# A routed MoE and attention kernel: dense batches get a place of their own, GpSimd makes the expert stages' rows, and all orders are planned anew

## The reference

```python
x = x + 0.5 * ffn(layernorm(x))      # stage A
x = x + attn(layernorm(x))           # stage B
x = x + 0.5 * ffn(layernorm(x))      # stage C, with the weights of stage A
```

## Time and profile before

| | |
|---|---|
| median of 3 runs | 1219.44 us (1216.77 to 1219.6) |
| profiled execution, its own time | 1225.29 us |
| its span, first to last instruction | 1223.5 us |
| PE, ACT, DVE, POOL busy | 94%, 78%, 59%, 55% |
| mean granted clock of PE | 0.946 of 2.4 GHz |
| DMA | 202 MB, mean 165 GB/s |

### The profile page before, as it was taken

How to read it: one execution, slowest core, us unless ns; L and a number is a source line. 1 busy time by engine, 2 the same in 40 slices (tenths; PEclk the granted TensorE clock), 3 DMA queues, 4 the chain that set the end, 5 groups by cost and what they waited for, 6 DMA issues and landing times.

```text
span 1223.5 us, 25810 instructions
## 1 busy us (share of the span) xinstructions
PE 1150.6 (94%) x8142; PEld 762.4 (62%) x8142; DVE 724.7 (59%) x2254; ACT 958.0 (78%) x2383; POOL 678.9 (55%) x768
## 2 busy tenths in 40 slices
PE   7989898999989989999999999999999999999896
PEld 3666576666666545676666665665766446667575
DVE  4775438666496745665555867555756636647245
ACT  4457748789898898997888888898989888888532
POOL 2035548537370887803876777881820884257646
PEclk8977888799999979999999998999999989999988
DMA  8056546456574115655677645567652144676872
GB/s 279 10 206 192 162 144 193 126 156 202 158 214 147 55 39 177 208 172 157 200 215 228 194 139 164 186 201 206 183 157 60 41 151 125 182 214 176 250 253 80
DMA packets 159882, 202.05 MB, mean 165 GB/s; under 512 B 16938, under 2 KB 103426, under 8 KB 159747
## 3 DMA queue, kind: packets, MB, share of 16 engines
q1 hardware_dynamic: 144196, 168.90, 44.8%
q0 software_dynamic: 15360, 31.49, 8.9%
q10 hardware_dynamic: 192, 0.02, 0.0%
HBM read 152.50 MB, written 47.84 MB: 164 GB/s over the span
## 4 chain that ended last, share of the span: by engine, by line
PE 68%; ACT 20%; DVE 4%; issue 3%; POOL 3%; DMA 2%; SPq 0%; POOLq 0%; ACTq 0%; DVEq 0%
PE psum L1568 63%; ACT probs L1173 7%; ACT psum L1182 6%; PE psum L1686 2%; DVE neg_m L1522 2%; POOL Y L1100 2%; ACT xnC L1138 1%; DMA wt<-packed 1%; ACT xnA L1138 1%; PE psum L1653 1%; ACT hg L1219 1%; POOL pause L1064 1%; ACT xnB L1138 1%; PE psum L1751 1%; ACT xg_T L1247 1%
## 5 line engine op out<-in xcount | busy, mean ns | idle before, releaser
L1522 DVE TENSOR_REDUCE neg_m<-psum 128x1 f32<-128x512 f32 x512 | 317.5, 685 | 189.4 <-PE psum L1568 188.9
L1568 PE MATMUL psum<-nat 32*128 32x512 f32 x2048 | 372.7, 667 | 2.8 <-ACT nat L1251 1.5
L1182 ACT ACTIVATE psum<-psum,neg_m 128x512 f32<-128x512 f32 x512 | 340.9, 681 | 34.5 <-DVE neg_m L1522 33.7
L1173 ACT ACTIVATE probs<-psum 128x512 f32<-128x512 f32 x512 | 266.0, 627 | 37.7 <-PE psum L1568 36.4
L1080 POOL DMA_INDIRECT slots_A<-xnA,posA x120 | 117.1, 976 | 197.9 <-DMA xs<-slots_A 64.3
L1100 POOL DMA_INDIRECT Y<-results_C,posC x120 | 115.4, 962 | 170.8 <-DMA results_C<-ys 130.9
L1064 POOL MEMSET pause<- 128x900 f32 x240 | 207.6, 865 | 0.1
L1568 PEld LDWEIGHTS psum<-xg_T,wt 128*128 128x128 f32 x1296 | 163.6, 200 | 49.7 <-ACT psum L1182 14.7
L1568 PEld LDWEIGHTS psum<-nat 32*128 32x128 f32 x2048 | 135.7, 191 | 91.7 <-issue 22.1
L1568 PE MATMUL psum<-xg_T,wt 128*128 128x128 f32 x1296 | 180.2, 290 | 7.4 <-DMA wt<-packed 3.3
L1568 PEld LDWEIGHTS psum<-wt,hg 128*128 128x128 f32 x1296 | 153.0, 193 | 27.6 <-ACT hg L1219 9.6
(11 more groups left out here) (190 smaller groups left out, 1374.9 us busy)
## 6 DMA issues: line engine op xcount, KB each, us to landing
wt<-packed SPq DMA_DIRECT2D x324, 320.0 KB, 4.0
xs<-slots_A SPq DMA_DIRECT2D x36, 256.0 KB, 4.3
results_A<-ys SPq DMA_DIRECT2D x36, 256.0 KB
xs<-slots_C SPq DMA_DIRECT2D x36, 256.0 KB, 4.4
results_C<-ys SPq DMA_DIRECT2D x36, 256.0 KB
X<-in_L_attn_x_dram SPq DMA_DIRECT2D x16, 256.0 KB, 8.0
out_dram<-X SPq DMA_DIRECT2D x16, 256.0 KB, 3.9
packed<-probs SPq DMA_DIRECT2D x1, 2560.0 KB, 9.0
```

What stands on the lines that cost most here:

```text
L1173: act.activation(probs[:, kt, j, :], at.banks()[j][:], ACT.Exp).then_inc(a_done, 1)
L1182: act.activation(at.banks()[j][:], at.banks()[j][:], ACT.Exp, bias=neg_m[:, g, n, j:j + 1], accum_out=sums[:, g, n, j:j + 1]).then_inc(S[" ...
L1522: V_.tensor_reduce(neg_m[:, g, n, j:j + 1], at.banks()[j][:], AX.X, ALU.max, negate=True).then_inc(S["r_done"], 1)
L1568: return nc.tensor.matmul(dst, w, m, start=start, stop=stop)
```

## The change

1. A dense batch's turned rows get a place of their own: `xT_F` has XF_RING + 1 places, the last for dense batches. A routed batch no longer waits for the dense one, and in the planner the dense batch takes `xTf_dense` instead of `xTf`.
2. In stages A and C the four tiles of rows are made by POOL, with `tensor_scalar` (times `rstd`, plus `shift`), and counted on a new semaphore `rows_done`. ACT keeps `scaled` for stage B alone. Who waited for `xn_done` of A or C now waits for `rows_done`: PE's `xTf`, ACT's next `norm`, DVE's next `scaled`.
3. The fill stands only between two `scat` or `gat` steps that follow each other on POOL. Where a row step stands between them, there is none: 212 fills in place of 240.
4. The planner's costs for `scat` and `gat` on POOL go from 3.4 to 2.4, the gap from 3.6 to 3.4, and the whole table of wanted times is new. So all lists are new.

```diff
-PERIOD, FIRST_B = 55.8, 402.13
+PERIOD, FIRST_B = 54.81, 448.4
...
-GAP = 3.6
+GAP = 3.4
...
+    "rows": ((("DVE", 1.0), ("POOL", 1.9)), 0.0),
...
-    "rank2": ((("PE", 1.0), ("DVE", 4.6)), 0.0), "scat": ((("POOL", 3.4),), 3.0),
+    "rank2": ((("PE", 1.0), ("DVE", 4.6)), 0.0), "scat": ((("POOL", 2.4),), 3.0),
...
-            steps[s, b, "xTf", 0].takes.append("xTf")
+            steps[s, b, "xTf", 0].takes.append("xTf_dense" if c == DENSE[s] else "xTf")
...
-                steps[s, c, "dh", EXPERTS * UNITS - 1].gives.append((0, "xTf"))
+                steps[s, c, "dh", EXPERTS * UNITS - 1].gives.append((0, "xTf_dense"))
...
-        xT_F = sb("xT_F", [P, XF_RING, TOKENS])
+        xT_F = sb("xT_F", [P, XF_RING + 1, TOKENS])
...
+        def xTf_place(s, b):
+            return XF_RING if CHUNK_OF[s][b] == DENSE[s] else xTf_turn[s, b] % XF_RING
...
-            def apart():
-
-                linked(pool.memset(pause[:], 0.0))
+            after_pair = {step for old, step in zip(order["POOL"], order["POOL"][1:]) if old[2] in ("scat", "gat")}
+
+            def apart(at):
+
+                if at.step in after_pair:
+                    linked(pool.memset(pause[:], 0.0))
...
+            def scaled(at):
+
+                s, b = at.stage, at.index
+                pool.wait_ge(S["shift_done"], at.count("shift_done"))
+                if b >= XN_RING:
+                    old = b - XN_RING
+                    if CHUNK_OF[s][old] == DENSE[s]:
+                        pool.wait_ge(a_full, at.count("a_full", "xTf", index=old))
+                    else:
+                        pool.wait_ge(scat_in[s][old % XN_RING], scattered(s, old))
+                for n in range(TILES):
+                    last = pool.tensor_scalar(xn[s][:, xn_place(s, b) + n, :], X[:, b % X_RING, n, :], rstd[s][:, n:n + 1],
+                                              shift[s][:, n:n + 1], ALU.mult, ALU.add)
+                last.then_inc(S["rows_done"], 1)
...
                 act.wait_ge(S["mv_done"], at.count("mv_done"))
-                wait(act, S["xn_done"], at.count("xn_done", "scaled", index=at.index - 1))
+                made = "xn_done" if at.stage == "B" else "rows_done"
+                wait(act, S[made], at.count(made, "scaled", index=at.index - 1))
...
-                pe.wait_ge(S["xn_done"], at.count("xn_done", "scaled", 0))
+                pe.wait_ge(S["rows_done"], at.count("rows_done", "scaled", 0))
```

More of the change, by code:

```diff
@@ L191 @@
     "y": ((("PE", 1.75), ("DVE", 0.65)), 0.0), "ystore": ((("SP", 0.48),), 4.2),
-    "gat": ((("POOL", 3.4),), 3.0), "comb": ((("DVE", 2.6),), 0.0), "store": ((("SP", 0.48),), 2.5),
+    "gat": ((("POOL", 2.4),), 3.0), "comb": ((("DVE", 2.6),), 0.0), "store": ((("SP", 0.48),), 2.5),
     "weights": ((("SP", 6.5),), 3.0), "b2": ((("PE", 1.9), ("ACT", 0.48)), 0.0), "cen": ((("PE", 2.0), ("DVE", 0.75)), 0.0),
@@ L213, in __init__ @@
         self.key, self.wanted, self.name = key, wanted, name
-        self.parts, self.lag = PARTS[name]
+        self.parts, self.lag = PARTS["rows" if name == "scaled" and key[0] != "B" else name]
         self.banks = GROUP if name in ("max", "rmax", "s") else 1
@@ L439, in plan @@
 def plan(steps):
-    free = {"xnA": XN_RING, "xnC": XN_RING, "xTf": XF_RING, "Y": Y_RING, "route": 1, "xs": XS_RING, "xg": XG_RING,
+    free = {"xnA": XN_RING, "xnC": XN_RING, "xTf": XF_RING, "xTf_dense": 1, "Y": Y_RING, "route": 1, "xs": XS_RING, "xg": XG_RING,
             "w": W_QUADS, "hg": HG_RING, "dhg": DHG_RING, "ys": YS_RING, "d": D_MOST, "a": A_MOST, "r": M_MOST}
@@ L677 @@
     "xn_done": {"scaled": 1},
+    "rows_done": {"scaled": 1},
     "lg_done": {"top1": 1},
@@ L733, in macaron_kernel @@
     comb_turn = {batch: i for i, batch in enumerate(combs)}
-    xTf_turn = {st[:2]: i for i, st in enumerate(st for st in order["PE"] if st[2] == "xTf")}
+    xTf_turn = {st[:2]: i for i, st in enumerate(st for st in order["PE"] if st[2] == "xTf" and CHUNK_OF[st[0]][st[1]] != DENSE[st[0]])}
     xTf_order = list(xTf_turn)
@@ L1125, in scaled @@
             def scaled(at):
-                s, b = at.stage, at.index
+                b = at.index
                 act.wait_ge(S["shift_done"], at.count("shift_done"))
-                if s != "B" and b >= XN_RING:
-                    old = b - XN_RING
-                    if CHUNK_OF[s][old] == DENSE[s]:
-                        act.wait_ge(a_full, at.count("a_full", "xTf", index=old))
-                    else:
-                        act.wait_ge(scat_in[s][old % XN_RING], scattered(s, old))
-                if s == "B":
-                    wait(act, d_full, at.count("d_full", "xT", index=b - 1))
+                wait(act, d_full, at.count("d_full", "xT", index=b - 1))
                 for n in range(TILES):
-                    last = act.activation(xn[s][:, xn_place(s, b) + n, :], X[:, b % X_RING, n, :], ACT.Identity,
-                                          bias=shift[s][:, n:n + 1], scale=rstd[s][:, n:n + 1])
+                    last = act.activation(xn["B"][:, n, :], X[:, b % X_RING, n, :], ACT.Identity,
+                                          bias=shift["B"][:, n:n + 1], scale=rstd["B"][:, n:n + 1])
                 last.then_inc(S["xn_done"], 1)
@@ L1230, in xTf @@
             def xTf(at):
-                i = xTf_turn[at.stage, at.index]
-                if i >= XF_RING:
-                    s0, b0 = xTf_order[i - XF_RING]
+                s, b = at.stage, at.index
+                if CHUNK_OF[s][b] != DENSE[s] and xTf_turn[s, b] >= XF_RING:
+                    s0, b0 = xTf_order[xTf_turn[s, b] - XF_RING]
                     act.wait_ge(d_full, counts["d_full", (s0, b0, "logits", 0)])
-                    if CHUNK_OF[s0][b0] == DENSE[s0]:
-                        act.wait_ge(a_full, counts["a_full", (s0, CHUNK_OF[s0][b0], "dh", EXPERTS * UNITS - 1)])
-                act.activation(xT_F[:, i % XF_RING, :], a_bank(at)[:], ACT.Copy).then_inc(a_done, 1)
+                act.activation(xT_F[:, xTf_place(s, b), :], a_bank(at)[:], ACT.Copy).then_inc(a_done, 1)
             def xg(at):
@@ L1351, in scaled @@
                 plus = shift[at.stage]
-                wait(dve, S["xn_done"], at.count("xn_done", index=at.index - 1))
+                made = "xn_done" if at.stage == "B" else "rows_done"
+                wait(dve, S[made], at.count(made, index=at.index - 1))
                 chain(V_.tensor_tensor(plus[:], mv[at.stage][:, :, 0], r[:], ALU.mult))
```

30 lines of the change are left out of this document (15 added, 15 removed).

## The result

| | before | after |
|---|---|---|
| median of the runs | 1219.52 us (4 runs) | 1189.89 us (4 runs, 1187.95 to 1193.21) |
| ratio | 1 | 0.9761, 95% interval 0.9729 to 0.9792 |
| the profiled execution, its own time | 1225.29 us | 1187.95 us |
| its span | 1223.5 us | 1186.2 us |
| mean granted clock in it | 0.946 | 0.978 |

The change makes the kernel faster by 29.6 us. The forecast was 1205 us, a gain of 14.5. The sign held, and the range (from 1188) just so; the gain is twice the forecast's.

The account below looks back on a forecast made before the run. PE was taken as the bound, with its 72.9 us of idle time and its time below full clock to be had. Terms +2.5 - 6 - 9 - 2 = -14.5 us gave 1205 us, range 1188 to 1225.

Parts of the forecast that it names:

- What bounds the kernel: Whole kernel: PE busy 94% of the span; to be had are its 72.9 us idle and its time below full clock.
- Part 1, price on POOL: Rows on POOL: 0.28 us per row tile, four 1.1 us (0.5 to 2.1); POOL stays near 690 us, free as load.
- Part 2, first batch: First rows wait behind POOL's setup, PE begins at 10.9 instead of 8.3 us, delay passed on: +2.5 us (1.9 to 3.5).
- Part 3, the start: Dense place, 60 to 110 us: two PE idles covered, first scatter and expert quads earlier: -6 us (0 to -19).
- Part 4, the middle: Behind 110 us: a third of the 26 us that ACT's rows hold in the chain, -9 us (0 to -26).
- Part 5, the tail: Before the tail's gathers: fewer xloads ahead of the store of chunk 11's last results, -2 us (0 to -4).
- The port: SBUF port shared by POOL and DVE: rows could hold up weighted sums, at most 2 us worse; counted as nothing.
- ACT was the bound in full: Rival, middle: all 26 us of ACT's rows in the chain come back, 1188 us; chance 0.14.
- Hidden anyway: Rival: ACT's work was already hidden, middle 0, start -4, tail 0, first batch +2.5: 1218 us, no change; chance 0.15.
- Rows stuck in POOL's line: Rival, behind the start: row steps wait behind POOL's gathers and scatters and stop PE, +23 us to 1228; chance 0.16.

Follow-up runs that it names:

- s_first_again: The changed kernel with batch 0's rows made inside POOL's setup, ahead of its affine_selects, run beside the change: 0.9726 of before, the change 0.9727.
- o_old_lists: The kernel before with its own lists, only the expert stages' rows moved from ACT to POOL, no fill where a row step stands between pairs: 0.9966 of before.
- l_act_load: The changed kernel, lists kept, with four unread 128x128 passes added on ACT behind each norm of A and C: 0.9838 of before.

## Why the prediction was right in sign and too small

**What bounds the kernel.** I named two things to be had, PE's idle time and the time below full clock, and then priced every part but one by idle time and chain. Idle time fell by 2.7 us of 72.9; the gain stands in the 80 us less at 1.2 GHz.

**Part 1, price on POOL.** 0.45 us where I took 0.28; inside the bounds, and nearest to the row I had called the upper one. It cost nothing: POOL is at 60%, and its rows wait for DVE's shift far more than anyone waits for them.

**Part 2, first batch.** +3.2 us at PE's first transposes, at 11.50 instead of 8.34 us, where I had +2.5 within 1.9 to 3.5. But I said that it is passed on to the end. In `s_first_again`, which takes it back, the product of span and clock falls by 3 us and the clock gives most of it away, so that no gain is seen at the end.

**Part 3, the start.** The mechanism was right in each step: rank1 and rank2 between the dense matmuls, both waits gone, scatter at 62.97 (forecast near 65), quads at 86.48. The size was 6, less 2.5 for the first batch, and some 13 came. The clock was in my bounds, up to 13.5 us "if all the clock loss goes too", and not in the sum. Time at 1.2 GHz up to 260 us fell from 71.6 to 34.1 us, worth 18.8, and its idle time there rose by 4.3. The idle time of 60 to 110 us stayed at 5.7 of 50 (5.9 before), because the wait for xnB came: what I had counted as won there was lost again, and the gain came by the clock.

**Part 4, the middle: the step that failed.** The step is the term for the clock, which I put at nothing. I took a third of the 26 us of ACT's rows in the chain, -9, from PE's idle time, and wrote that the trace can't say whether one order drifts less than another. The idle part was about right: PE's idle time from 260 to 1110 us fell from 28.2 to 21.3, 7 us, and `o_old_lists` gets 5.5 of them with no new order at all. But the middle gave some 24. The missing term is the clock: 44.4 us at 1.2 GHz became 3.4, worth 20.5. It was in the earlier trace rows, a clock of 0.98 over 900 us, which is 18 us to be had, beside 30.7 of idle time, and I gave it no term. `o_old_lists` shows that the lighter ACT alone does not bring it, and `l_act_load` that the new lists keep only part of it once ACT has half of its load again, 30.7 us at 1.2 GHz. It takes both. The new order I called a part of this term and gave no price. The planner's own lengths, 1196.8 and 1175.5 us, could have given one: 21 us, though for costs that differ a little.

**Part 5, the tail.** Nothing came, where I had -2 within 0 to -4: 66.5 us from the last `wo` add in both, and the first gather equally far from the end.

**The port.** The weighted sums of A take 349 ns, 346 before, beside 56 us of rows on POOL. The rule of the Trainium skill, "SBUF — State Buffer", section "SBUF: two separate sides", would let the new rows hold them up, or be held up by them. The trace agrees where the two meet, which is at five row passes and ten sums. There it is mostly the rows that wait: 0.47 to 0.83 us instead of 0.44, 0.8 us in all.

```profile
L1123 POOL TENSOR_SCALAR xnC<-X,rstdC,shiftC x64: 437/442/833, 160.3 to 1128.3; 128x128 f32<-128x128 f32 x64
```

The three times are the least, the median and the most, in ns. Counting nothing was right here, since the two seldom meet.

**The rivals.** "ACT was the bound in full" gave 1188 us, nearly the 1190 that was measured, but that is luck: it wanted 26 us of PE's waiting back, and 7 came. "Hidden anyway" is close to what the load alone is worth in the old lists, 4 us. "Rows stuck in POOL's line" did not come: behind the first batch PE waits for rows twice, 3.7 us. One rival was missing, that new lists change the clock.

**What stays open.** What makes the clock fall. `o_old_lists` and the change have nearly the same idle time in the middle (22.7 and 21.3 us), with 41.0 and 3.4 us at 1.2 GHz. A second profile of the same change has 13.7 us there.

What stands ahead of the falls is known in part. In the six us ahead of each of the seven falls in the middle of before, PE waited 0.44 to 2.36 us in six, five times for ACT. Only one in seven of all such stretches at full clock holds as much waiting. Over the middles of all 20 profiles it is 83 falls of 115. The first of the seven, at 422.0 us, stands right behind a wait for rows that ACT no longer makes in the change. The wait, then the stretches ahead of the fall, at the lower level and behind it:

```profile
421.37 0.63 PE L1653 MATMUL psum<-ident,xnC 128*128 128x128 f32 x4 [2.36 <-ACT xnC L1138]
...
416.00:422.00 6.00, 3.64 (x31) 1.70 (x25) 5.53 (x17) 5.76 (x14) 4.91 (x6) 1.00 0.22 66
422.00:425.40 3.40, 3.40 (x19) 2.63 (x20) 1.79 (x6) 3.06 (x9) 2.80 (x3) 0.50 0.13 41
425.40:431.00 5.60, 5.60 (x36) 2.84 (x31) 2.73 (x6) 5.60 (x15) 4.68 (x6) 1.00 0.15 47
```

But a wait is not enough. Of PE's ten waits of 0.8 us or more at full clock in the middle of before, five were followed by a fall within 7 us, and in the change one of eight. Why so few in the new order, these runs don't tell. Fillers raised the clock in the one place where they were tried. No run made the clock alone better or worse in the middle, so it was not forced that the lists act through it.

## What to carry to other kernels

Multiply each execution's span by its mean granted clock before you explain a gain. If the products are equal, as 1159 and 1160 here, the gain stands in the clock, and neither the sum of the idle time nor the chain shows it. Price the time below full clock as a term of its own, half of what stands at the lower level, beside the idle time. Then look at what TensorE waited for right ahead of each fall. Here such a wait stood ahead of six falls in seven, though that it brings them isn't shown.

Where a planner makes the order, a part that is tried with a table made for another structure is charged for the table: 2 to 6% here, as much as the whole change or more. Fit a table for each variant with the same effort, and more than one, since fitted tables of one structure spread by 2%.

Compute the planner's length again from the kernel that runs, not from the fit. Here it ranked all but close neighbours, and the one kernel that seemed to break the rule had another gap than its fit. Run the best few.

## What was not expected of the hardware

- The same 8142 matmuls took 1116 us of PE's time in one order and 1151 in the other, and the granted clock makes up the difference (0.978 and 0.946: busy time times clock is 1091 and 1088 us).
- Repeated runs of one kernel differ in the same way: the seven of the change in one group have spans from 1186.5 to 1196.6 us, clocks from 0.978 to 0.968, and products from 1158 to 1161.
- A POOL tensor_scalar of 128x128 with two numbers per partition takes 0.44 to 0.45 us, four of them 1.73 us, where an affine_select of the same size took 0.28 and ACT's pass 0.51.
- The clock fell seven times in the middle of the kernel before, where no wait of PE was longer than 2.36 us.
